# Both groups of score products side by side on TensorE, and the exponential ahead of the evictions on ScalarE

## The reference, cut to what matters

```python
x = x + tanh(g_xattn[0]) * xattn0(layernorm(x), ctx)   # 16 heads of 16, softmax over 256 context tokens
x = x + tanh(g_ffn[0])   * ffn0(layernorm(x))          # 8 experts + 1 shared, top 4, computed densely
x = x + tanh(g_xattn[1]) * xattn1(layernorm(x), ctx)   # as xattn0, with scores clipped to +-10000
x = x + tanh(g_ffn[1])   * ffn1(layernorm(x))          # 8 experts of 1024 hidden, top 2, routed

# attention of either layer
attn = softmax(einsum('bhnd,bhmd->bhnm', q * hd ** -0.5, k))
out = einsum('bhnm,bhmd->bhnd', attn, v).reshape(B, N, C) @ wo + bo
```

## Time and profile before

| | |
|---|---|
| median of 3 runs | 1029.55 us (1026.08 to 1035.4) |
| profiled execution | 1034.0 us, span 1032.1 us |
| mean granted clock of TensorE | 0.902 of full |
| PE busy | 923.3 us (89%), 6385 products |
| PE weight loads busy | 737.4 us (71%) |
| DVE busy | 749.5 us (73%) |
| ACT busy | 486.5 us (47%) |
| POOL busy | 242.0 us (23%) |

### The profile page before, as it was taken

The page is one execution under the profiler, slowest core; times in us unless marked ns, Lnnn a source line. Parts: engine busy times, 40 slices in busy tenths (PEclk is TensorE's granted clock), DMA queues, the critical chain, the costliest instruction groups (busy, mean ns, idle before and its releaser), DMA issues.

```text
span 1032.1 us, 18031 instructions
## 1 busy us (share of the span) xinstructions
PE 923.3 (89%) x6385; PEld 737.4 (71%) x6385; DVE 749.5 (73%) x1494; ACT 486.5 (47%) x842; POOL 242.0 (23%) x390
## 2 busy tenths in 40 slices
PE   5578899999999999999989788786599999999995
PEld 3355677777767666776766555554599999999995
DVE  2345676777676768988888889757688888888882
ACT  2125544443444443443433444431276666677662
POOL 5011210120201000111010133320434444444433
PEclk9557999999999999999999866765599999999998
DMA  5766896254161444547363873430577667777642
GB/s 153 151 123 123 170 209 106 65 90 80 41 104 43 69 102 86 105 116 136 100 133 94 222 167 90 117 87 22 190 241 235 206 208 225 228 232 233 208 144 30
DMA packets 129866, 141.52 MB, mean 137 GB/s; under 512 B 12561, under 2 KB 122281, under 8 KB 129649
## 3 DMA queue, kind: packets, MB, share of 16 engines
q1 hardware_dynamic: 119296, 127.59, 49.4%
q0 software_dynamic: 8832, 12.25, 5.5%
q10 hardware_dynamic: 1648, 0.53, 0.3%
HBM read 109.45 MB, written 30.36 MB: 135 GB/s over the span
## 4 chain that ended last, share of the span: by engine, by line
PE 66%; DVE 19%; issue 4%; ACT 3%; POOL 2%; DMA 2%; SPq 1%; POOLq 0%; DVEq 0%; ACTq 0%
PE bank L966 12%; PE bank L802 9%; PE by_query L950 7%; PE by_key L950 6%; DVE rowmax L1295 5%; PE bank L812 5%; PE value_bank L744 4%; PE bank L650 4%; PE by_query L707 3%; PE bank L693 3%; DVE probs L1320 3%; PE by_key L726 2%; PE bank L659 2%; PE bank L771 2%; DMA lower<-lower 2%
## 5 line engine op out<-in xcount | busy, mean ns | idle before, releaser
L1295 DVE TENSOR_REDUCE rowmax<-by_query 128x4 f32<-128x1024 f32 x128 | 155.6, 1216 | 20.2 <-PE by_query L707 20.1
L1102 ACT ACTIVATE probs<-by_key 128x1024 f32<-128x1024 f32 x128 | 130.7, 1021 | 46.3 <-PE by_key L726 43.3
L1788 POOL TENSOR_SCALAR rstd<-moments 128x2 f32<-128x2 f32 x32 | 10.5, 328 | 526.5 <-DVE moments L1254 526.5
L1848 POOL DMA_INDIRECT out_x<-x,token_i x46 | 78.2, 1699 | 146.6 <-ACT x L1205 136.7
L966 PE MATMUL bank<-w_hi,h_hi 128*128 128x256 f32 x368 | 104.1, 283 | 0.0
L966 PE MATMUL bank<-w_lo,h_hi 128*128 128x256 f32 x368 | 104.1, 283 | 0.0
L966 PE MATMUL bank<-w_hi,h_lo 128*128 128x256 f32 x368 | 104.1, 283 | 0.0
L707 PE MATMUL by_query<-stack_k,stack_q 48*128 48x256 f32 x512 | 70.5, 357 | 30.6 <-DVE rowmax L1295 30.1
L1135 ACT ACTIVATE act_gate<-bank 128x256 f32<-128x256 f32 x72 | 27.6, 383 | 141.5 <-PE bank L802 139.0
L707 PEld LDWEIGHTS by_query<-stack_k,stack_q 48*128 48x128 f32 x512 | 42.9, 206 | 70.0 <-DVE rowmax L1295 39.2
L1320 DVE SCALAR_TENSOR_TENSOR probs<-probs,lower 128x1024 f32<-128x1024 f32 x64 | 78.1, 1220 | 11.5 <-DMA lower<-lower 6.7
(11 more groups left out here) (242 smaller groups left out, 2143.7 us busy)
## 6 DMA issues: line engine op xcount, KB each, us to landing
w<-in_L_ffn_W SPq DMA_DIRECT2D x46, 1024.0 KB, 8.9
lower<-lower SPq DMA_DIRECT2D x64, 256.0 KB, 5.4
stack_k<-qk SPq DMA_DIRECT2D x96, 128.0 KB, 5.2
stack_q<-qk SPq DMA_DIRECT2D x96, 128.0 KB, 6.8
qk<-hi SPq DMA_DIRECT2D x31, 256.0 KB, 2.6
qk<-lo SPq DMA_DIRECT2D x31, 256.0 KB, 2.7
rows<-w_gate SPq DMA_DIRECT2D x8, 264.0 KB, 4.8
x<-in_x SPq DMA_DIRECT2D x8, 256.0 KB, 6.4
```

Of the source, the lines that this page charges most:

```text
L1102: ac.activation(probs[i % 4][:, :, :, :].rearrange("p k h s -> p h k s"), by_key[:, :, :].rearrange("p h (k s) -> p h k s", k=2), ACT.Exp) ...
L1295: dv.tensor_reduce(rowmax[u % 2][:, :, p, :], by_query[:, :, :].rearrange("p h (t s) -> p h t s", t=TT), AX, ALU.max).then_inc(sem.max_don ...
L1848: po.indirect_dma_start(out[:, :], bass.IndirectOffsetOnAxis(ap=token_i[:, n:n + 1].bitcast(U32), axis=0), ysb[i % 3][:, t, :], None, comp ...
```

## The change

On PE the plan's first half moves behind the key-side scores and the values, so that the order of a slot becomes query-side scores, key-side scores, values, first half, second half. On ACT the exponential moves ahead of the plan's first half. DVE, POOL and SP keep their order, and no instruction is added or taken away.

```diff
@@ PE's loop
             v, q = divmod(g - base(0), PAIRS)
             if 0 <= v < UNITS:
                 scores_by_query(v, q)
-            for stage, n in PLAN[2 * g]:
-                if stage in stages:
-                    stages[stage](n)
             u, p = divmod(g - base(0) - LAG, PAIRS)
             if 0 <= u < UNITS:
                 scores_by_key(u, p)
             u, p = divmod(g - base(0) - LAG - 3, PAIRS)
             if 0 <= u < UNITS and p % 2 == 0:
                 weigh_values(u, p // 2)
-            for stage, n in PLAN[2 * g + 1]:
+            for stage, n in PLAN[2 * g] + PLAN[2 * g + 1]:
                 if stage in stages:
                     stages[stage](n)
@@ ACT's loop
         for g in range(SLOTS_IN_ALL):
-            for stage, n in PLAN[2 * g - 1] + PLAN[2 * g]:
+            for stage, n in PLAN[2 * g - 1]:
                 if stage in stages:
                     stages[stage](n)
             u, p = divmod(g - base(0) - LAG, PAIRS)
             if 0 <= u < UNITS:
                 exponentials(u, p)
+            for stage, n in PLAN[2 * g]:
+                if stage in stages:
+                    stages[stage](n)
```

## The result

The changed kernel takes 1045.5 us (median; 1039.6 to 1048.7, 4 runs), the kernel before beside it 1029.9: ratio **1.0141, interval [1.0073, 1.0208]**. A second comparison of the same two gave 1.0131 [1.0082, 1.0180]. It is slower by 1.3 to 1.4%. The forecast was 1024 us; the range ended at 1042. Rival C, the values' wait for the clip, had said 1047.

What follows compares the result with a forecast made beforehand. PE was taken to bound slots 44 to 115 (124 to 512 us); a 19.5 us gain less 4.4, 2.8, 4.3, 1.5 and 1.0 gave -5.5 us, so 1024 us from 1029.55; range 1008 to 1042.

Steps and rivals of the forecast that it cites:

- Rival C: Values' wait for the clip in slots 95 to 157 replaces the saved borders: 17 x 1.45 us, 1047 us; chance 0.15.
- The border and what it saves: Slots 44 to 115: fewer changes between half-height score products and full-height ones, 0.39 us per slot, gain 19.5 us.
- (a): Slots 43 to 113: router products now wait for ACT's copy of the transposes, 0.4 to 0.9 us in six, 4.4 us.
- (b): Gate/up waits longer for the PSUM bank of the query projection, 0.74 us more in slots 50, 82, 90; 2.8 us altogether.
- (c): Eleven rearranged slots where DVE sets the pace: PE's saving returns as longer waits for maxima, 4.3 us.
- (e): ACT's exponential ahead of the first half's evictions only fills a wait: 0 cost; PE needs that order.
- (f): At the end, earlier scores and values set against late short stages in slots 141, 145, 157; 0, from -5 to +5.
- (d): Layer 1 values lose their cover and wait for DVE's clip: four slots at 0.38 us, 1.5 us.
- (g): Full-rate stage: new waits beside the router's thin products may bring half-rate dips on PE, 1.0 us, ends 0 and 15.
- D: Clock rival: nine more half-rate dips at 1.7 us, 1039 us; sign, granted clock below 0.97; chance 0.1.
- B: Rival: the savings stay, new waits only eat DVE idle time they themselves make; 1010 us; chance 0.2.

Runs made afterwards that it cites:

- e8: Changed kernel with DVE's clip moved ahead of its first-half work, PE and ACT as changed; 1028.9 us, ratio 0.9964 to the kernel before.
- f1: Kernel before, PE and ACT untouched, with DVE's clip moved ahead of its first-half work; ratio 0.9995 to the kernel before.
- e3: Changed kernel with the values put back behind the first half, the two score groups still together; ratio 0.9955 to the kernel before.
- e5: Changed kernel with the values put back behind the first half from slot 92 on only; 1032.9 us, ratio 0.9981 to the kernel before.
- e10: e8 with the values put back behind the first half in the eight router slots; 1027.2 us, ratio 0.9938 to the kernel before.
- e12: Changed kernel with unread PE products in the router and clip waits, cut to the waits' size; 1038.2 us, ratio 1.0059 to the kernel before.
- e6: Change applied only in slots below 92, the kernel before's order from there on; ratio 0.9968 to the kernel before.
- e11: Changed kernel with unread PE products in the router and clip waits, up to seven per clip wait; 1046.0 us, ratio 1.0095 to the kernel before.

## Why the prediction was wrong

**The border and what it saves: right.** Forecast 0.39 us a slot; slot 68 took 3.45 instead of 3.85, and 48, 60, 92 and others fell by 0.38 or 0.39; 65, 75 and 105 by 0.2. "Issue" ahead of the key-side scores went from 73 times to 5. PE's busy time from slot 44 to 116 fell by 7.5 us in spite of 17 us more at half rate; 17 us at 1.65 lost in every 3.4 are 8.3, so 15.8 us without them, against 19.5 forecast: somewhat too much.

**(a) Router: right.** PE waits for the copy 3.3 us in four places, 0.73 to 0.84 each, and the waits of slots 43 and 103 grew too. Slots 73, 83 and 113 grew by 0.68 or 0.69, where 0.9 less the border's 0.39 would be 0.5. **(b) Query bank: about right.** The wait of slot 50 went from nothing to 0.67 us, slot 90's from 0.27 to 0.85, slot 122's from 0.28 to 0.86; forecast 0.74 more. **(c) DVE stretches: about right.** Waits for the maxima 30.1 to 33.6 us in the whole run, with slot 77 from 0.41 to 1.57. **(e) ACT: right**; it waits more (86.1 us for the key-side scores instead of 43.3), and PE's own wait for the exponential fell from 3.1 to 0.6 us. **(f) End: near**, +1.9 us of slot 145 to the end.

**(d) The clip: the step that failed.** Forecast: "I take four at the row's value, for in the others DVE is far ahead: 1.5 us". The waits were in slots 95 (1.71 us), 99 (0.78), 103 (0.17), 107 (0.28), 109 (1.25) and 115 (1.72): 5.9 us, 5.1 more than before. Behind slot 115 I had set nothing, and in slots 116 to 145 they come to 11.0 us against 3.4. I asked where the clip stood in the old trace, as if PE's order left it there: in slot 119 itself the wait went from 0.38 to 0.85. DVE's first half waits for products that PE now issues behind both score groups, and the clip is queued behind it: in slot 108 it starts 4.56 us after the slot's first product, in the trace of before 3.88. Wait and cover changed at one stroke: the values came earlier (slots 95, 103, 107, 115), and the clip later, which alone made the growth in 99, 109 and 119, where the first half is empty and I had expected nothing new.

**(g) The clock: the term mis-sized most.** Forecast 1.0 us, ends 0 and 15. Slots 44 to 116 have 20.5 us at half rate, six times 3.4, against 3.4, 0 and 0 before: at 1.65 lost in every 3.4, some 9.4 us lost. I had looked for dips only at the router's thin products. They came behind a wait for the clip too: slot 109 had two.

The sum up to slot 116 then closes: forecast -5.5, measured +6.7 (mean of three traces). The clip was 3.6 too small and the half rate 8.4, which is 12.0 of the 12.2 missed. The other terms' errors nearly cancel: PE's idle time beside the clip's grew by some 8 us where (a), (b) and (c) said 11.5, and the saving was some 3.5 short. The +5.5 behind slot 116 is rival C's place too, and e8 takes it away (133.8 us); but f1 is as short there (132.5 us), and e3 and e5 differ by 10.5 us there at the same order from slot 92 on, so how much of it is the clip's alone stays open.

**The rivals.** C was right in place and direction, and by the sign that the prediction set (more than 10 us of wait for the clip; 21.3 us measured). Its 1047 was right in size by luck in part: 14.8 us more of waiting rather than 24.7 of queueing, with half rate, of which it said nothing, filling in; and its count of 17 is met by 17 waits, but not in the same slots, as 99, 109 and 119 are among them and have no first half. D's clock is a large part of the loss, though by D's own sign (below 0.97 between 124 and 500 us; measured 0.98) it isn't D. B fell. With the clip early and the router covered, e10 gains 5.6 us; that this is the size of the forecast's 5.5 is no support for it, as it is another kernel.

## What to carry to other kernels

When work is moved on one engine so that a consumer comes earlier, ask of its producer not when it ran in the old trace but what it is queued behind, and whether that too depends on what was moved; then move the producer to the head of its queue in the same edit. Price a new wait on TensorE twice: its own length, and a possible stretch at half rate behind it, and take more than one trace, for such stretches come and go at the same order. To part the two, fill the wait with unread products, but measure one first and fill no more than the wait.

## What the runs showed of the hardware

- On TensorE, in a nearly full stream (PE busy 91% of slots 92 to 116 in the changed kernel), stretches of 3.4 us at 1.2 GHz appeared, each making its slot 1.6 to 1.7 us longer (slots 104, 109 and 114, changed kernel against e12). Some stand behind waits of 0.7 to 1.7 us: slot 109's 6.8 us came in six of six traces with a bare wait of 1.25 us or more and in none of two with the wait filled. A wait isn't enough: e6 and e8 had the router's waits below slot 92 and no half rate.
- Two fp32 score groups of 48 and 50 rows side by side cost 0.39 us less than with full-height products between them (slots 48, 60, 68 and 92).
- An unread fp32 product of 256 columns took 0.44 us (e11, seven in 3.1 us); where such products outlasted the wait, the slot grew by the rest, 1.4 us in slot 95.
